# A sixteen-sequence linear-attention and local-attention kernel on one core: x in two buffers, the attention norm written over the turned rows, linear scores issued in fours, the layer input turned whole, set-up and main work in one block

## The chip, the cores and the metric

The kernel runs on one core of a Trainium2 chip. The metric is the device time of one execution in microseconds (us); smaller is better. The engines are named as the profile names them: PE (matrix products and the transposes done with them), PEld (its weight loads), DVE, ACT, POOL, and SP, which here only issues transfers.

## What is computed

The input x is 16 sequences of 512 rows and 128 columns. The reference, cut to what matters:

```python
# linear attention, 16 heads of 8
q, k, v = rope(x @ Wq.T), rope(x @ Wk.T), x @ Wv.T
q, k = elu(q) + 1, elu(k) + 1
y = causal_sum(q, k, v) / max(q . cumsum(k), 1e-6)
x = x + layernorm(y @ Wo.T)             # sandwich: x is normed ahead of it, too
# two layers, 8 heads of 64, windows of 64 looking one window back
for l in range(2):
    h = shift_token(x)                  # second half of the columns one row later
    q, k, v = split(h @ wqkv[l])
    q, k = rotary(l2norm(q) * qs, l2norm(k) * ks)
    x = x + softmax(mask(8 * q @ k.T)) @ v @ wo[l]
    h = layernorm(shift_token(x)) * g + b
    a, g = split(h @ w1[l] + b1)
    x = x + (a * gelu(g)) @ w2[l] + b2
```

The output is the residual after attention plus the norm of the layers' result.

## The kernel before, in words

Each sequence is four tiles (j = 0 to 3) of 128 rows. Its work is cut into steps, such as `yt` (four transposes of the normed x, L640), `aqkv` (L647), `as` (linear attention's scores, L679), `awo` (its output product, L705), `h` (the shifted layer input turned, L716 to L721), `qkv` (nine f16 products of 512 columns, L732), `qkt` (q and k turned, L744), `s` (window scores, L753 and L759), `pt` (probabilities turned, L771), `o` (L787), `wo` (L798), `w1` (L827) and `w2` (L838). A step has its part on other engines: copies out of the banks on ACT, rope, masks and norms on DVE, additions and normalising on POOL.

Nothing is scheduled while the kernel runs. A table `TIMES` gives every step of a sequence a number on each engine, `STARTS` gives each of the 16 sequences an offset, some 14,133 apart, and `order_of` sorts the sums: that is the order in which an engine issues. So four or five sequences are in flight, at different stages. Each engine takes its steps strictly in this order and waits on semaphores for what they need. The eight banks of 512 columns go to PE's steps by the table `HOLD` (`banks_of`), and `take` makes PE wait until the bank's last user has released it.

Set-up is a block of its own (L481 to L563): 38 loads on SP behind one semaphore, memsets on POOL, then, when all has landed, weights split into two f16 halves (ACT L533, DVE L545), the rope tables scaled (DVE L557), masks cast, and linear attention's weights turned (PE L525). Only when every engine has ended that block does the second block begin, with the first load of x (L588).

Around the change:

- `load` (L584) writes the one buffer `x_in`, so it waits until the sequence before has been kept (`x_kept`) and normed (`act_ln["mid"]`). Then come `ln_in` on DVE (L1047), `rstd` on POOL, `norm_in` on ACT (L867) into `y_rows`, and `yt` on PE.
- `norm_attn` (L1055) writes attention's normed output into `y_rows` too, and `add_mid` (L1253) adds it to x. So `norm_in` of a sequence waits for `add_mid` of the one before.
- `scores_linear` (L672) takes a bank and issues a product, four times.
- `h` (L709) makes the row shift on PE: one product that zeroes a column (L716), four that shift the upper half of the columns (L719), four transposes of the lower half (L721). One copy on ACT (L908) and one subtraction on DVE (L1131) then write the two f16 halves of `h_cols`.
- `expand` (L1271) writes one of two buffers `la_qexp`.

Of the kernel before, what the change touches and what calls it, by code (L numbers as in the profile page):

```python
# [91 lines left out]
class Step:  # L92
# [8 lines left out]
    def name(self):  # L101
# [3 lines left out]
STARTS = [8839, 22968, 37104, 51237, 65372, 79508, 93645, 107777, 121914, 136050, 150187, 164318, 178448, 192583, 206718, 220840]  # L105
TIMES = {
    "tensor": {
        "yt": [[4430]],
        "aqkv": [[5379, 5741, 5887, 6259]],
        "at": [[6260, 7486, 7515, 12974]],  # L110
        "aq": [[6500, 7904, 12992, 14314]],
        "as": [[9594, 9957, 14446, 14942]],
        "ao": [[10473, 10563, 14977, 15227]],
        "awo": [[15262]],
        "h": [[17736], [35934]],
        "qkv": [[17805, 20226, 20589, 21185], [38794, 39614, 41261, 43323]],
        "qkt": [[20484, 21053, 21367, 23845], [42226, 42333, 43672, 44789]],
# [8 lines left out]
    },  # L126
    "vector": {
        "ln_in": [[3336]],
        "arope": [[4897, 5228, 5494, 7780]],
        "phi": [[5339, 7394, 8144, 12251]],  # L130
        "den": [[6519, 8903, 12441, 14291]],
        "mask": [[10206, 11028, 15093, 15325]],
        "ln_attn": [[15539]],
        "norm_attn": [[16843]],
        "ln_mid": [[17151]],
        "h": [[18039], [38031]],
        "ss": [[18745, 20244, 21725, 23553], [40963, 41947, 43215, 43739]],
        "rope": [[19117, 21242, 22076, 22957], [41018, 42210, 43239, 44970]],
        "max": [[21946, 22977, 23802, 25207], [43513, 45053, 45539, 46335]],
# [43 lines left out]
        "r_ffn": [[29895], [51024]],  # L183
        "b2": [[29689], [53617]],
        "r_out": [[60936]],
        "add_out": [[67247]],
    },
    "sync": {
        "load": [[3648]],
# [1173 lines left out]
```

## Time and profile before

| | |
|---|---|
| median of 3 runs | 1835.49 us (1835.01 to 1836.9) |
| profiled execution, its own time | 1839.22 us |
| its span, first to last instruction | 1836.7 us, granted PE clock 0.971 |
| PE busy | 1641.0 us, 89% of the span |
| ACT, DVE, POOL busy | 1367.3, 1329.3, 1285.8 us |
| chain that ended last, by engine | PE 70%, ACT 12%, POOL 7%, issue 6%, DVE 3% |

The profiled execution is 3.7 us above the median of the runs, and 2.5 us of its time lie outside its span. Busy time says how much of the span an engine worked; a matrix product's end is modelled, so neighbouring products overlap in the rows, and what a step costs PE is best read from its start to the start of the next step.

### The profile page before, as it was taken

The numbers are of one execution on the slowest core, as the hardware profiler recorded it, in microseconds if no ns is written. First come the engines' busy times: TensorE is split into PE (matmuls) and PEld (weight loads), VectorE is DVE, ScalarE is ACT, GpSimd is POOL, SyncE is SP. The second block draws the span as 40 slices with busy tenths as digits, with TensorE's granted clock in tenths as the row PEclk, the third lists the DMA queues.
The fourth block names the chain that finished last, engine by engine and source line by source line (L and its number), as shares of the span: only waits on it lengthen the run. The fifth ranks groups of instructions, "written<-read, shape, count | busy, mean of one in ns | idle before, by whom it ended". The sixth has DMA issues, their size and how long they took to land.

```text
span 1836.7 us, 51372 instructions
## 1 busy us (share of the span) xinstructions
PE 1641.0 (89%) x18212; PEld 1149.2 (63%) x18340; DVE 1329.3 (72%) x3471; ACT 1367.3 (74%) x4277; POOL 1285.8 (70%) x1715
## 2 busy tenths in 40 slices
PE   0677989999999999999999999999999999998875
PEld 0344666666667666666666666666667666666653
DVE  2465777877777787877778787777777787776552
ACT  1264768787887878798887878787787878788663
POOL 1263777777777887777777787777777887777562
PEclk9888999999999999999999999999999999999986
DMA  3000001011111011111111011111101011111001
GB/s 117 12 16 19 22 23 25 18 36 30 36 28 28 19 34 27 31 36 30 36 28 28 19 31 30 31 36 28 39 22 31 22 25 36 30 31 30 19 21 29
DMA packets 58135, 54.52 MB, mean 30 GB/s; under 512 B 7538, under 2 KB 42780, under 8 KB 57756
## 3 DMA queue, kind: packets, MB, share of 16 engines
q1 hardware_dynamic: 57884, 51.25, 11.0%
q8 instruction: 149, 2.44, 0.5%
q14 instruction: 102, 0.84, 0.2%
HBM read 13.48 MB, written 8.39 MB: 12 GB/s over the span
## 4 chain that ended last, share of the span: by engine, by line
PE 70%; ACT 12%; POOL 7%; issue 6%; DVE 3%; DMA 0%; POOLq 0%; ACTq 0%; DVEq 0%; SPq 0%
PE bank L732 10%; PE bank L787 7%; PE bank L759 7%; PE bank L798 5%; PE bank L744 5%; PE bank L771 5%; PE bank L838 4%; PE bank L827 4%; PE bank L679 4%; PE bank L695 3%; PE bank L753 2%; PE bank L719 2%; ACT probs L959 2%; ACT probs_t L853 2%; POOL qk_rows L1308 2%
## 5 line engine op out<-in xcount | busy, mean ns | idle before, releaser
L959 ACT ACTIVATE probs<-bank,s_low 128x128 f32<-128x128 f32 x1024 | 360.1, 384 | 60.7 <-DVE s_low L1171 60.6
L1308 POOL TENSOR_TENSOR qk_rows<-qk_rows,qk_tmp 128x512 f32<-128x512 f32 x256 | 328.2, 1282 | 16.6 <-DVE qk_tmp L1159 15.8
L1321 POOL TENSOR_TENSOR probs<-probs,s_rden 128x512 f32<-128x512 f32 x256 | 263.5, 1050 | 68.1 <-DVE s_rden L1180 68.1
L732 PE MATMUL bank<-wqkv_sb,h_cols 128*128 128x512 f16 x1152 | 281.2, 388 | 7.9 <-ACT probs_t L853 2.6
L1311 POOL TENSOR_TENSOR qk_rows<-qk_rows,qk_rnorm 128x512 f32<-128x512 f32 x256 | 268.7, 1050 | 20.1
L959 ACT ACTIVATION_READ_ACCUMULATOR probs<-bank,s_low 128x1 f32 x1024 | 229.0, 224 | 0.0
L1156 DVE TENSOR_TENSOR qk_rows<-bank,rope 128x512 f32<-128x512 f32 x256 | 174.4, 681 | 39.2 <-POOL qk_rows L1311 35.4
L1126 DVE TENSOR_TENSOR room<-bank,const 128x512 f32<-128x512 f32 x256 | 158.7, 683 | 57.8 <-PE bank L679 56.2
L732 PEld LDWEIGHTS bank<-wqkv_sb,h_cols 128*128 128x128 f16 x1152 | 108.2, 99 | 142.7 <-issue 22.7
L853 ACT ACTIVATE probs_t<-bank 128x512 f32<-128x512 f32 x256 | 140.9, 598 | 67.9 <-PE bank L771 65.2
L1142 DVE TENSOR_REDUCE qk_sum<-qk_sq 128x16 f32<-128x1024 f32 x128 | 155.1, 1212 | 46.2 <-ACT qk_sq L918 44.2
L1171 DVE TENSOR_REDUCE s_low<-bank 128x4 f32<-128x512 f32 x256 | 164.3, 684 | 30.6 <-PE bank L759 30.6
L1159 DVE TENSOR_TENSOR qk_tmp<-bank,rope 128x512 f32<-128x512 f32 x256 | 174.3, 681 | 0.0
L918 ACT ACTIVATE qk_sq<-bank 128x512 f32<-128x512 f32 x256 | 144.4, 618 | 22.9 <-PE bank L732 22.2
L798 PE MATMUL bank<-wo_sb,o_cols 128*128 128x128 f32 x1024 | 141.0, 281 | 19.4 <-DVE room L1126 12.5
L744 PE MATMUL bank<-const,qk_rows 128*128 128x128 f32 x1024 | 140.8, 281 | 15.4 <-POOL qk_rows L1311 12.6
L798 PEld LDWEIGHTS bank<-wo_sb,o_cols 128*128 128x128 f32 x1024 | 129.5, 195 | 38.1 <-DVE room L1126 24.9
L771 PE MATMUL bank<-const,probs 128*128 128x128 f32 x1024 | 142.5, 280 | 8.8 <-POOL probs L1321 6.8
L787 PE MATMUL bank<-probs_t,v_even 128*64 128x64 f32 x2048 | 133.2, 228 | 17.6 <-ACT probs_t L853 10.1
L759 PEld LDWEIGHTS bank<-k_cols,q_cols 64*64 64x64 f32 x4096 | 112.3, 134 | 55.5 <-issue 55.5
L759 PE MATMUL bank<-k_cols,q_cols 64*64 64x128 f32 x4096 | 143.4, 278 | 0.0
L827 PE MATMUL bank<-h_cols,w_sb 128*128 128x512 f16 (+1 forms) x576 | 139.6, 386 | 2.1 <-ACT h_cols L990 0.9
(154 smaller groups left out, 3650.6 us busy)
## 6 DMA issues: line engine op xcount, KB each, us to landing
v_even<-v_rows SPq DMA_DIRECT2D x224, 128.0 KB, 2.3
x_in<-in_L_attn_x SPq DMA_DIRECT2D x16, 256.0 KB, 3.2
kept_rows<-x_in SPq DMA_DIRECT2D x16, 256.0 KB, 2.3
x_back<-kept_rows SPq DMA_DIRECT2D x16, 256.0 KB, 3.0
out<-x_back SPq DMA_DIRECT2D x16, 256.0 KB, 2.4
room<-in_constants SPq DMA_DIRECT2D x1, 1024.0 KB
hidden<-in_L_ffn_wqkv SPq DMA_DIRECT2D x1, 768.0 KB
qk_rows<-in_L_ffn_wqkv SPq DMA_DIRECT2D x1, 768.0 KB
```

The costliest lines, as they stand in the source:

```text
L732: mm = pe.matmul(to[:, :], h_cols[st.l][:, x_half, st.j * P:(st.j + 1) * P], wqkv_sb[:, st.l, w_half, w * INNER:(w + 1) * INNER], start=(n ...
L744: mm = pe.transpose(to[:, c * P:(c + 1) * P], qk_rows[st.l][:, a, w, c * P:(c + 1) * P], ident)
L759: mm = pe.matmul(to[half][w * WIN:(w + 1) * WIN, c * P:(c + 1) * P], q_cols[st.l][rows, a, c, w * WIN:(w + 1) * WIN], k_cols[st.l][rows, c ...
L771: mm = pe.transpose(to[:, c * P:(c + 1) * P], probs[st.l][:, half * PAIRS + c, :], ident)
L787: mm = pe.matmul(to[half * DH:(half + 1) * DH, c * P + w * WIN:c * P + (w + 1) * WIN], values[l][:, a, head * DH:(head + 1) * DH], probs_t ...
L798: mm = pe.matmul(to[:, 0:D], o_cols[st.l][:, c * P:(c + 1) * P], wo_sb[:, st.l, c, :], start=(c == 0), stop=(c == PAIRS - 1))
L827: mm = pe.matmul(to[0:n, :], w1_sb[:, st.l, w_half, half * HID + at_:half * HID + at_ + n], h2_cols[:, x_half, :], start=(p == 0), stop=(p ...
L853: return act.activation(to, of, ACT.Copy)
L959: act.activation(probs[st.l][:, n, :], bank[b[half]][:, c * P:(c + 1) * P], ACT.Exp, bias=s_low[st.l][:, a, n:n + 1], accum_out=s_sum[st.l ...
L1308: pool.tensor_tensor(rows(w), rows(w), qk_tmp[l][:, w, :], ALU.add).then_inc(pool_qk.of(st), 1)
L1311: pool.tensor_tensor(heads64(rows(w)), heads64(rows(w)), qk_rnorm[l][:, a, w * HEADS:(w + 1) * HEADS].unsqueeze(2).to_broadcast([P, HEADS, ...
L1321: pool.tensor_tensor(probs[l][:, mine, :], probs[l][:, mine, :], s_rden[l][:, a, mine].unsqueeze(2).to_broadcast([P, PAIRS, P]), ALU.mult) ...
```

## The change

What it does:

- `x_in` becomes two buffers, by the sequence's parity; `load` waits for the sequence two back.
- `norm_attn` writes into `y_cols` (seen by rows, `att_rows`), which `awo` has just read; `norm_in` then waits only for the last `yt`, and the copy that fills `y_cols` (`yt` on ACT) waits for the `add_mid` before.
- `scores_linear` takes its four banks first and then issues the four products; a step never gets one bank twice. `la_qexp` becomes one buffer, and `expand` waits for the tile before.
- `h` is four transposes of the whole 128 columns. The row shift is made where the bank is read: two copies on ACT and two subtractions on DVE, each of 64 partitions, the upper ones one column further. Column 0 is zeroed once.
- There is one block. x is loaded first, then what linear attention needs (5 loads, semaphore `first_loaded`), then layer by layer (`loaded[l]`). Splitting weights and scaling tables are called from within the engines' orders, in the first sequence. PE waits for `ready[l]` ahead of each layer's first `qkv`. Each engine sets the starting values of its own semaphores. The memsets write only what needs a zero.
- `STARTS`, `TIMES` and `HOLD` have new numbers throughout.

```diff
-STARTS = [8839, 22968, 37104, 51237, 65372, 79508, 93645, 107777, 121914, 136050, 150187, 164318, 178448, 192583, 206718, 220840]
+STARTS = [-1084, 13059, 27198, 41340, 55477, 69615, 83756, 97894, 112036, 126177, 140319, 154457, 168599, 182734, 196875, 211009]
...
-            b = min(range(BANKS), key=lambda b: (free[b], b))
+            b = min(set(range(BANKS)) - set(banks[step.name()]), key=lambda b: (free[b], b))
...
-        x_in = sb("x_in", [P, NT, D])
+        x_in = sb("x_in", [P, 2, NT, D])
...
+        att_rows = y_cols[:, :].rearrange("p (j d) -> p j d", j=NT)
...
-        la_qexp = room[:, 0:1024].rearrange("p (a s q) -> p a s q", a=2, s=SLOTS)
+        la_qexp = room[:, 0:512].rearrange("p (s q) -> p s q", s=SLOTS)
...
+        def start_signals(engine, mine):
+            for sig in every:
+                if sig.name.split("_")[0] in mine:
                     for sem in sig.sems:
-                        sp.sem_inc(sem, sig.start())
+                        engine.sem_inc(sem, sig.start())
...
-                    sp.wait_ge(*x_kept.at(st, back=1))
-                    sp.wait_ge(*act_ln["mid"].at(st, back=1))
-                    sp.dma_start(x_in[:, :, :], rows_of(x, st)).then_inc(x_loaded.of(st), 16)
+                    sp.wait_ge(*x_kept.at(st, back=2))
+                    sp.wait_ge(*act_ln["mid"].at(st, back=2))
+                    sp.dma_start(x_in[:, st.n % 2, :, :], rows_of(x, st)).then_inc(x_loaded.of(st), 16)
...
+                start_signals(sp, ("x", "out", "v", "sh"))
+                for at, (_, st) in enumerate(order["sync"]):
+                    if at > 0:
+                        run(st)
+                        continue
+                    sp.dma_start(x_in[:, 0, :, :], rows_of(x, st)).then_inc(x_loaded.of(st), 16)
+                    load_first()
+                    for l in range(DEPTH):
+                        load_layer(l)
+                    sp.wait_ge(zeroed, ZEROED)
...
                     pe.wait_ge(*pool_qexp.at(st))
+                    to = [take(banks, g) for g in range(GROUPS)]
                     for g in range(GROUPS):
-                        to = take(banks, g)
...
-                    pe.matmul(to[DH:P, 0:1], ident[:, DH:P], cst("causal")[:, 0:1], start=True, stop=True)
                     for j in range(NT):
-                        n = min(P, T - 1 - j * P)
-                        pe.matmul(to[DH:P, j * P + 1:j * P + 1 + n], x_res[st.l][0:n, j, DH:D], ident[0:n, 0:n],
-                                  start=True, stop=True)
-                        mm = pe.transpose(to[0:DH, j * P:(j + 1) * P], x_res[st.l][:, j, 0:DH], ident)
+                        mm = pe.transpose(to[:, j * P:(j + 1) * P], x_res[st.l][:, j, :], ident)
...
+                start_signals(pe, ("pe",))
+                pe.wait_ge(first_loaded, 16 * FIRST_LOADS)
+                for n in range(4):
+                    mm = pe.transpose(bank[0][:, n * D:(n + 1) * D], la_rows[:, n * D:(n + 1) * D], ident)
+                mm.then_inc(turned, 1)
+                pe.wait_ge(la_ready, 2)
                 for _, st in order["tensor"]:
+                    if st.kind == "qkv" and st.n == 0 and st.j == 0:
+                        pe.wait_ge(ready[st.l], READY[st.l])
...
                 def yt(st, b):
                     act.wait_ge(*pe_yt.at(st))
+                    act.wait_ge(*pool_xmid.at(st, back=1))
...
                 def norm_in(st, b):
-                    act.wait_ge(*pool_xmid.at(st, back=1))
+                    act.wait_ge(*pe_yt.at(st, back=1))
...
-                    copy(h_cols[st.l][:, 0, :], bank[b[0]][:, :]).then_inc(act_h.of(st), 1)
+                    copy(to[0:DH, 0, :], bank[b[0]][0:DH, :]).then_inc(act_h.of(st), 1)
+                    copy(to[DH:P, 0, 1:T], bank[b[0]][DH:P, 0:T - 1]).then_inc(act_h.of(st), 1)
...
-                    normed(st, "attn", lambda j: bank[b[0]][:, j * D:(j + 1) * D], lambda j: y_rows[:, j, :])
+                    normed(st, "attn", lambda j: bank[b[0]][:, j * D:(j + 1) * D], lambda j: att_rows[:, j, :])
...
-                    dve.tensor_tensor(h_cols[st.l][:, 1, :], bank[b[0]][:, :], h_cols[st.l][:, 0, :],
+                    dve.tensor_tensor(to[0:DH, 1, :], bank[b[0]][0:DH, :], to[0:DH, 0, :],
+                                      ALU.subtract).then_inc(dve_h.of(st), 1)
+                    dve.tensor_tensor(to[DH:P, 1, 1:T], bank[b[0]][DH:P, 0:T - 1], to[DH:P, 0, 1:T],
                                       ALU.subtract).then_inc(dve_h.of(st), 1)
...
+                    if st.name() == ("den", 0, 1, 0):
+                        lower_weights(0)
+                    if st.name() == ("mask", 0, 0, 0):
+                        turn_tables(0)
+                        turn_masks()
+                    if st.name() == ("mask", 0, 3, 0):
+                        lower_weights(1)
+                    if st.name() == ("ln_mid", 0, 0, 0):
+                        turn_tables(1)
...
-                    pool.wait_ge(*pe_as.at(st, back=2))
-                    pool.tensor_tensor(la_qexp[:, a, :, :],
+                    pool.wait_ge(*pe_as.at(st, back=1))
+                    pool.tensor_tensor(la_qexp[:, :, :],
```

`lower_weights`, `turn_tables` and `turn_masks` on DVE and `halve` on ACT hold the operations of the old set-up block unchanged, with semaphores. ACT calls `halve(0)` after `av` of the first sequence's last tile and `halve(1)` after its first `ao`.

On SP, the end of set-up and the first steps, before:

```order
L502 DMA room<-in_L_ffn_k_scale 128x64
L481 UNCONDITIONAL_BRANCH
L579 UNCONDITIONAL_BRANCH
L588 DMA x_in<-in_L_attn_x 128x4x128
L592 DMA kept_rows<-x_in 128x4x128
L588 DMA x_in<-in_L_attn_x 128x4x128
```

and now the start of the program on SP (its line numbers are the changed kernel's):

```order
L581 DMA x_in<-in_L_attn_x 128x4x128
L554 DMA o_cols<-in_L_attn_Wq 128x128
L554 DMA o_cols<-in_L_attn_Wk 128x128
L554 DMA o_cols<-in_L_attn_Wv 128x128
L554 DMA o_cols<-in_L_attn_Wo 128x128
L555 DMA const<-in_constants 128x708
L559 DMA hidden<-in_L_ffn_wqkv 128x1536
```

The first x went out last, behind the block's end; now it goes first, and five loads later PE may begin.

On PE, the layer input's `h` in the middle of the program, before (scores of a window ahead of it; the pair L719, L721 stands four times):

```order
L753 MATMUL bank<-mask_h,ident_h 128x512 x2
L759 MATMUL bank<-k_cols,q_cols 64x128 x16
L716 MATMUL bank<-const 64x1
L719 MATMUL bank<-const,x_res 64x128
L721 MATMUL bank<-const,x_res 64x128
```

and now (L711 and L717 are the window's scores, L609 `aqkv`, L729 `pt`, L679 `h`, L756 `wo`):

```order
L711 MATMUL bank<-mask_h,ident_h 128x512 x2
L717 MATMUL bank<-k_cols,q_cols 64x128 x16
L609 MATMUL bank<-w_la,y_cols 128x384
L729 MATMUL bank<-const,probs 128x128 x8
L679 MATMUL bank<-const,x_res 128x128 x4
L756 MATMUL bank<-wo_sb,o_cols 128x128 x4
```

Nine instructions became four, and `aqkv` of the next sequence (L609), which stood behind `h`, now stands ahead of it.

On PE, behind the first `qkv` of layer 0, before (L640 is `yt` and L647 `aqkv` of the next sequence, L771 `pt`):

```order
L732 MATMUL bank<-wqkv_sb,h_cols 128x512 x9
L640 MATMUL bank<-const,y_rows 128x128 x4
L771 MATMUL bank<-const,probs 128x128 x8
L647 MATMUL bank<-w_la,y_cols 128x384 x2
L787 MATMUL bank<-probs_t,v_even 64x64 x2
```

and now (L690 is `qkv` of tiles 0 and 1, L785 `w1`, L616 and L626 `at`, L756 `wo`, L729 `pt`, L609 the last `aqkv`; one `o` and then `qkt` of tile 0 follow):

```order
L690 MATMUL bank<-wqkv_sb,h_cols 128x512 x18
L785 MATMUL bank<-h_cols,w_sb 128x512 x6
L616 MATMUL bank<-la_phi,const 128x128
L626 MATMUL bank<-const,la_phi 128x128
L785 MATMUL bank<-h_cols,w_sb 128x512 x6
L756 MATMUL bank<-wo_sb,o_cols 128x128 x4
L729 MATMUL bank<-const,probs 128x128 x8
L785 MATMUL bank<-h_cols,w_sb 85x512 x6
L609 MATMUL bank<-w_la,y_cols 128x384
```

Between `qkv` and `qkt` of tile 0, `yt`, one `pt` and three `aqkv` have gone; all else that stood there still does.

## Rows read from the trace of the kernel before

**Rows 1.** Windows: stretch, length, busy us per engine, granted clock, DMA share, GB/s.

```profile
303.00:407.10 104.10, 99.71 (x1141) 70.64 (x1148) 80.36 (x211) 84.70 (x268) 78.74 (x106) 1.00 0.11 27
...
1447.60:1552.50 104.90, 99.82 (x1141) 70.64 (x1148) 82.00 (x215) 85.02 (x268) 80.03 (x108) 1.00 0.12 29
```

**Rows 2.** Waits of PE from 511 to 927 us: total, times, longest.

```profile
PE bank L640 <- ACT y_rows L864: 4.1, 4, 1.0
PE bank L798 <- DVE room L1126: 3.3, 4, 0.8
```

**Rows 3.** Timeline of PE, 600 to 720 us: start, length, instruction; both `h`.

```profile
627.01 0.28 PE L716 MATMUL bank<-const 128*64 128x1 f32 x2
...
629.50 0.34 PE L787 MATMUL bank<-probs_t,v_even 128*64 128x64 f32 x4
...
639.59 0.60 PE L815 MATMUL bank<-const,h_rows 128*128 128x128 f32 x4
640.12 1.14 PE L679 MATMUL bank<-room,la_qk_cols 32*128 32x512 f32 x8
...
691.97 0.28 PE L716 MATMUL bank<-const 128*64 128x1 f32 x2
...
694.36 1.06 PE L798 MATMUL bank<-wo_sb,o_cols 128*128 128x128 f32 x8
```

**Rows 4.** Groups by form, ACT and DVE, 511 to 927 us: busy, mean ns, idle.

```profile
L853 ACT ACTIVATE h_cols<-bank 128x512 f16<-128x512 f32 x8 | 4.8, 597 | 10.1 <-PE bank L721 10.1
L1134 DVE TENSOR_TENSOR h_cols<-bank,h_cols 128x512 f16<-128x512 f32 x8 | 5.5, 688 | 1.0 <-ACT h_cols L853 1.0
L1000 ACT ACTIVATE hidden<-bank,b_cols 128x512 f32<-128x512 f32 x16 | 10.1, 684 | 0.1
L1000 ACT ACTIVATE hidden<-bank,b_cols 85x512 f32<-85x512 f32 x8 | 5.5, 684 | 0.5
```

**Rows 5.** The start: one window, and two rows of the timeline.

```profile
0.00:10.00 10.00, 0.00 (x0) 0.00 (x0) 0.00 (x0) 1.28 (x1) 7.21 (x19) 1.00 0.84 291
...
35.68 0.38 SPq L588 DMA_DIRECT2D x_in<-in_L_attn_x  x1
...
43.24 1.11 PE L640 MATMUL bank<-const,y_rows 128*128 128x128 f32 x4 [19.20 <-ACT y_rows L864]
```

**Rows 6.** Timeline of set-up on DVE.

```profile
24.42 1.76 DVE L545 SCALAR_TENSOR_TENSOR wqkv_sb<-hidden,wqkv_sb 128x1536 f16<-128x1536 f32 x1 [1.25 <-ACT wqkv_sb L533]
...
26.09 0.86 DVE L545 SCALAR_TENSOR_TENSOR w_sb<-room,w_sb 128x682 f16<-128x682 f32 x1
...
30.31 4.39 DVE L557 SCALAR_TENSOR_TENSOR rope<-room 128x64 f32<-128x64 f32 x32
```

**Rows 7.** Timeline of DVE in the first sequence's linear attention.

```profile
57.74 4.88 DVE L1126 TENSOR_TENSOR room<-bank,const 128x512 f32<-128x512 f32 x8 [2.12 <-PE bank L679]
...
77.38 0.89 DVE L1027 BATCH_NORM_STATS2 ln_stats_attn<-bank 128x6 f32<-128x128 f32 x4 [3.11 <-PE bank L705]
```

**Rows 8.** Timeline of DVE, the norm of a later sequence's x.

```profile
693.11 0.87 DVE L1027 BATCH_NORM_STATS2 ln_stats_in<-x_in 128x6 f32<-128x128 f32 x4 [2.21 <-DMA x_in<-in_L_attn_x]
```

**Rows 9.** Timeline of PE and POOL behind the first `qkv` of layer 0.

```profile
699.11 1.04 PE L771 MATMUL bank<-const,probs 128*128 128x128 f32 x8
700.11 1.53 PE L647 MATMUL bank<-w_la,y_cols 128*128 128x384 f32 x4
...
702.65 0.91 PE L647 MATMUL bank<-w_la,y_cols 128*128 128x384 f32 x2
...
707.66 1.04 POOL L1311 TENSOR_TENSOR qk_rows<-qk_rows,qk_rnorm 128x512 f32<-128x512 f32 x1
...
711.96 1.04 PE L744 MATMUL bank<-const,qk_rows 128*128 128x128 f32 x8
```

**Rows 10.** One line of DVE: ns min/median/max over the run.

```profile
L1098 DVE SCALAR_TENSOR_TENSOR la_phi<-la_tb,la_phi x64: 361/519/1099, 50.4 to 1582.9; 128x256 f32<-128x256 f32 x64
```

**Rows 11.** Timeline of PE, a linear score step with a wait inside.

```profile
664.73 1.66 PE L679 MATMUL bank<-room,la_qk_cols 32*128 32x512 f32 x8
```

More of the change, by code:

```diff
@@ L102, in name @@
         return self.kind, self.l, self.j, self.n
-STARTS = [8839, 22968, 37104, 51237, 65372, 79508, 93645, 107777, 121914, 136050, 150187, 164318, 178448, 192583, 206718, 220840]
+STARTS = [-1084, 13059, 27198, 41340, 55477, 69615, 83756, 97894, 112036, 126177, 140319, 154457, 168599, 182734, 196875, 211009]
 TIMES = {
     "tensor": {
[L108 to L117, printed above, removed]
[8 rows of a table removed]
+        "yt": [[1158]],
+        "aqkv": [[2489, 2532, 2791, 6884]],
+        "at": [[4747, 8646, 9544, 9563]],
+        "aq": [[7014, 9242, 9578, 10422]],
+        "as": [[9363, 9420, 11127, 12264]],
+        "ao": [[9396, 9564, 14266, 14691]],
+        "awo": [[14736]],
+        "h": [[17531], [37133]],
+        "qkv": [[18557, 18868, 21223, 21826], [37717, 37818, 38228, 40867]],
+        "qkt": [[21050, 22007, 22211, 23528], [38284, 40531, 40869, 43385]],
[8 rows of a table added]
@@ new lines @@
+        "arope": [[4092, 4623, 5005, 7413]],
+        "phi": [[4675, 7364, 11296, 11633]],
+        "den": [[6477, 10514, 12784, 13983]],
+        "mask": [[10890, 11635, 15176, 15779]],
+        "ln_attn": [[17077]],
+        "norm_attn": [[17729]],
+        "ln_mid": [[17773]],
+        "h": [[18820], [39085]],
+        "ss": [[19735, 21000, 22082, 23183], [40148, 41353, 42710, 44412]],
+        "rope": [[20422, 21284, 22434, 24117], [40364, 41804, 43140, 44685]],
+        "max": [[22303, 24407, 25017, 26815], [43977, 44803, 46012, 46919]],
@@ L184 @@
-        "b2": [[29689], [53617]],
-        "r_out": [[60936]],
-        "add_out": [[67247]],
+        "r_in": [[937]],
+        "ar": [[2562, 2652, 2782, 6648]],
+        "aden": [[4262, 7986, 10959, 11311]],
+        "expand": [[7221, 9672, 11320, 11580]],
+        "r_attn": [[15507]],
+        "add_mid": [[16105]],
+        "r_mid": [[16458]],
+        "norms": [[18318, 19562, 20652, 21694], [38807, 39374, 40127, 43031]],
+        "normalize": [[18387, 20433, 20720, 23582], [39045, 39580, 42128, 43176]],
@@ L1010, in _, with halve @@
                 on_gelu = True
+                def halve(l):
+                    act.wait_ge(loaded[l], 16 * LOADS[l])
+                    for whole, halves in ((whole_wqkv[l], wqkv_sb[:, l, :, :]), (whole_w1[l], w1_sb[:, l, :, :])):
+                        act.activation(halves[:, 0, :], whole, ACT.Copy, scale=W_SCALE).then_inc(halved, 1)
+                start_signals(act, ("act",))
+                act.wait_ge(zeroed, ZEROED)
                 for _, st in order["scalar"]:
@@ new lines, in turn_tables @@
+                def turn_tables(l):
+                    for w, (names, by) in enumerate(((("q_cos", "q_sin"), QK_SCALE), (("k_cos", "k_sin"), 1.0))):
+                        sc = qk_scale[:, l, w, :].rearrange("p (a b) -> p a b", a=2)
+                        for c, name in enumerate(names):
+                            scales = sc[:, ::-1, :] if c else sc
+                            for j in range(NT):
+                                dve.scalar_tensor_tensor(
+                                    out=rope[:, l, 2 * w + c, j * DH:(j + 1) * DH].rearrange("p (a b) -> p a b", a=2),
+                                    in0=cst(name)[:, j * DH:(j + 1) * DH].rearrange("p (a b) -> p a b", a=2),
+                                    scalar=by, in1=scales, op0=ALU.mult, op1=ALU.mult).then_inc(ready[l], 1)
```

310 lines of the change are left out of this document (146 added, 164 removed), and 32 rows, old and new, of tables (HOLD, TIMES).

## The prediction

> **What bounds the kernel now.** I read the windows first, then PE's waits, then the timeline at the places that the change touches. In the windows, twelve sequences in a row, from 303 to 1552 us, take 104.0 to 104.9 us each, and PE is busy 99.7 to 99.8 us of that at a granted clock of 1.00, which is the upper of its two levels, 2.4 GHz [rows 1]. ACT works some 85 us of the same stretch, DVE 80 to 82, POOL 79 to 80 [rows 1]. So in the steady part PE's own work sets the pace. The 4.3 us in which it idles consist of small waits, and two of them have names: 1.0 us per sequence until the normed x of the next sequence is there, 0.8 us until DVE has masked linear scores ([rows 2], where each stands for four sequences). A microsecond taken from PE here is a microsecond per sequence, until another wait takes its place. The two ends of the run are another matter. PE turns the first x at 43.24 us [rows 5], after a set-up block and one load; there, chains of latency decide.
>
> **The change part by part.**
>
> *Start.* Now x is issued at 35.68 us and turned 7.56 us later [rows 5]. In the changed order x is SP's first transfer, and five loads follow it. Together they are 0.87 MB (256 KB of x, four weights of 64 KB, 128 rows of 708 constants), or 3.0 us at the 291 GB/s of the first ten microseconds [rows 5]. To the 7.56 us I add these 3.0, then 1.1 for turning linear attention's weights (the same four transposes took 1.11 cold [rows 5]) and 0.8 for two copies of them by DVE, an estimate from an ACT copy of as many columns [rows 4]. If x is issued at about 1.5 us, the first turn comes at 14: a lead of 29 us. I hold 26 to 31 possible, since what the engines spend on setting their semaphores has no row.
>
> *Set-up work within the first sequence.* It is no longer ahead of everything, but DVE still has to do it. Ahead of the first `h` stand both splits, 2 x (1.76 + 0.86), and half of the tables, 2.2 [rows 6], with some 1.5 us of small casts: 8.9 us. DVE waits in that stretch anyway, 2.1 us for the first scores and 3.1 us for `awo` [rows 7]. If the work fills these two holes, 3.7 us remain on the path; at best nothing does, at worst all 8.9. The second half of the tables comes after `ln_mid`, beside POOL's and ACT's share of that norm, and I cost it at nothing; without that cover it would be 2.2 us, once. I take 4, so the lead at the first `h` is **25 us** (17 to 31).
>
> One row bears on how long this work takes beside POOL: an operation of DVE with two inputs from SBUF takes 0.36 us at least, 0.52 in the middle and 1.10 at most over the run [rows 10]. The Trainium skill (SBUF — State Buffer, "Who interferes with whom") says that such an instruction contends with a POOL instruction that reads SBUF, the later one being blocked; the spread agrees. By that rule the moved operations, which had POOL idle beside them, would take longer now, by the middle of the row 0.16 us for each of about 20: 3 us more, inside the bounds above.
>
> *The layer input.* Nine PE instructions took 2.49 and 2.39 us from their first to the next step's first; four whole transposes of the same kind take 0.53 [rows 3]. That is 1.96 + 1.86 = 3.8 us of PE time less per sequence. In the twelve full periods all of it counts: 46 us. The other four sequences' eight steps fall where PE has gaps. There the path also gets what the split adds: a second copy on ACT, 0.60, and a second subtraction on DVE, 0.69 [rows 4]. Half the partitions do not halve these: ACT took 684 ns on 128 and on 85 of them [rows 4]. So each of the eight saves between 0.6 and 1.9 us; I take 1.2, together 10. Sum **56 us** (51 to 61). In the steady part the extra 1.2 us of ACT and 1.4 of DVE per sequence lie inside their 19 and 22 us of slack [rows 1]; what is queued behind them is in the next but one item.
>
> *Two buffers for x.* The wait of 1.0 us per sequence on PE [rows 2] ends a chain: DVE waited 2.2 us for x itself [rows 8], then come the norm on POOL and ACT. With a second buffer the load may go out one sequence earlier, and `norm_in` no longer waits for `add_mid`. In the new order `ln_in` also stands ahead of `ln_attn` of the sequence before. I expect this wait to go: 12 x 1.0 = **12 us** (0 to 12). The copy into `y_cols` now waits for `add_mid` instead, and holds `aqkv`; on PE, about ten steps stand between `awo` and that.
>
> *Handing over to `qkt`.* The order was laid out anew, and one place got tighter. Behind the first `qkv` of layer 0, POOL ended its normalising at 707.66 + 1.04 = 708.70, and PE came to `qkt` at 711.96 [rows 9]: 3.3 us to spare. From between them `yt`, one `pt` and three `aqkv` have been taken. These are 0.5 us (four transposes, as above), 1.0 (699.11 to 700.11) and 2.3 (two in 1.53, one in 0.91, overlaps taken off) [rows 9]: 3.8 us. What was 3.3 early is now 0.5 late, and ACT's second copy, which stands ahead of the squares, adds 0.6. I charge 1.2 us per sequence, 12 x 1.2 = **14 us**. Nothing at all is the lower bound, since POOL and ACT were reordered too; 3.8 + 0.6 = 4.4 us, 53 in all, is the upper one, if today's spare time is gone for another reason.
>
> *Linear scores.* Four products cost 1.14 us [rows 3]; a step that had to wait inside took 1.66 [rows 11]. Taking the banks first moves such a wait ahead of the products and changes nothing in the sum. The single `la_qexp` lets POOL's next expansion start only after the products; on PE, two other steps and an `ao` stand between two such steps, so I cost it at nothing. Without that cover it would be one addition-sized POOL operation, about a microsecond.
>
> **Sum.** -25 - 56 - 12 + 14 = -79 us against the profiled execution's 1839.2, so 1760. The median of the runs lies 3.7 us below that execution; I forecast **1756 us**, with 1738 to 1775 as this case's own range.
>
> **The rivals.**
>
> *The new handovers bind.* If `qkt` comes late by the full 4.4 us in every period, 3.2 us more than charged, the time is 1756 + 12 x 3.2 = 1794. For it speaks that ACT and POOL are 82% and 77% busy, so a chain through both seldom has its shortest length. Against it speaks that today's spare time is measured, 3.3 us [rows 9], and would have to be lost to other causes.
>
> *PE's other waits shrink as well.* Of 4.3 us of idle time per sequence 3.3 remain without the x wait. If half of that goes and the 1.2 us do not come, the time is 1756 - 12 x 2.8 = 1722. For it: PE's named waits now are all for masks, copies and norms that a new order can place earlier. Against it: the second copy and subtraction, and fewer PE steps to hide behind.
>
> *Four banks at once are not to be had: slower than before.* PE stands still until the fourth bank is free, with everything queued behind it. There are 64 such steps, 4 per sequence. It decides from a mean wait of 79 / 64 = 1.2 us. Its price at worst is a whole set of masks, 4.88 / 2 = 2.4 us [rows 7]: 64 x 2.4 = 156, so 1912. For it: the 0.5 us inside one step [rows 11] and the 0.8 us behind masks [rows 2] are waits of this kind. Against it: they are 1.3 us per sequence today, not 5.
>
> *The start gains nothing.* If the five first loads land only with all the rest, which is issued behind them on the same queue, PE begins no earlier in effect, and the 25 us are lost: 1781.
>
> **How the numbers follow.** Forecast 0.63, handovers 0.15, shrinking waits 0.13, banks 0.04, start 0.05. The range takes in the first two rivals' times and the start's, with a few microseconds beyond each: 1718 to 1800. A measurement of this kernel can tell about 0.2%, 3.7 us, from no change. Only the banks' case lies above that; the handovers would have to cost 6.4 us more per period than I charged to come near it. So 0.95 for faster, 0.01 for the same, 0.04 for slower.
>
> **What would show it.** Right: a first turn of x at 12 to 17 us; a period of 99 to 102 us with PE busy about 96; `h` at about 0.5 us on PE; no wait for the normed x; a new wait of a microsecond at the first `qkt`. Wrong: a period still near 104 with PE busy 96 (the work went, the time did not); PE waiting ahead of linear scores; a first turn after 20 us.

## The result and the profile after

The changed kernel takes **1748.56 us** (median of 4 runs, 1748.41 to 1750.26) against 1835.66 before (4 runs): a ratio of 0.9527, 95% interval 0.951 to 0.9543, 87.1 us less. The forecast was 1756, the range 1718 to 1800. The profiled execution took 1748.4, of which its span is 1746.6.

The page of the kernel after, its first and its fourth part (busy time of each engine; the chain that ended last, by engine):

```profile
PE 1575.0 (90%) x17892; PEld 1110.9 (64%) x18020; DVE 1375.7 (79%) x3503; ACT 1383.1 (79%) x4309; POOL 1292.7 (74%) x1717
...
PE 38%; ACT 27%; POOL 14%; issue 10%; DVE 10%; DMA 0%; POOLq 0%; SPq 0%; ACTq 0%; DVEq 0%
```

PE had 70% of that chain before; now ACT, POOL and DVE hold half of it. Windows of the kernel after, two of eleven equal ones in a row (columns as in [rows 1]):

```profile
337.37:438.22 100.85, 96.33 (x1121) 68.52 (x1128) 84.80 (x217) 85.88 (x270) 80.56 (x108) 1.00 0.12 31
...
1345.87:1446.72 100.85, 95.98 (x1120) 68.38 (x1127) 85.35 (x218) 85.46 (x271) 80.27 (x107) 1.00 0.12 31
```

Against [rows 1]: the period went from 104.1 to 100.85, PE's busy time from 99.7 to 96.0, its idle time from 4.4 to 4.8 (both traces lack the same few of PE's records; the last section has what that does to these two). PE's timeline after, both `h` (compare [rows 3]):

```profile
447.35 0.63 PE L679 MATMUL bank<-const,x_res 128*128 128x128 f32 x4 [0.52 <-ACT x_res L831]
447.92 1.16 PE L756 MATMUL bank<-wo_sb,o_cols 128*128 128x128 f32 x8
...
481.56 0.66 PE L679 MATMUL bank<-const,x_res 128*128 128x128 f32 x4
482.26 0.38 PE L711 MATMUL bank<-mask_h,ident_h 128*128 128x512 bf16 x1
```

From `h` to the next step it is 0.57 and 0.70 us, where it was 2.49 and 2.39. PE's waits from 438.1 to 943.4, five periods (compare [rows 2], which are four):

```profile
PE bank L690 <- DVE h_cols L1117: 4.4, 5, 1.1
PE bank L745 <- DVE room L1106: 4.0, 5, 0.8
PE bank L711 <- DVE room L1106: 2.8, 4, 0.8
PE bank L702 <- POOL qk_rows L1341: 2.5, 5, 0.5
PE bank L679 <- ACT x_res L831: 2.1, 4, 0.5
...
PE bank L641 <- DVE x_att L1168: 1.9, 5, 0.4
PE bank L641 <- ACT k_cols L819: 1.7, 5, 0.3
```

The wait for the normed x is gone. New are 0.9 us per sequence for the lower half of `h_cols` (`qkv`, L690), 0.5 for the normalised q and k (`qkt`, L702), and 0.7 for banks ahead of linear scores (`as`, L641). The masks (`room`) now hold up two steps, L745 and L711.

The start, from the timeline of several engines (compare [rows 5]):

```profile
1.79 0.44 SPq L581 DMA_DIRECT2D x_in<-in_L_attn_x  x1
...
12.88 1.28 ACT L831 ACT_TABLE_LOAD   x1 [12.88 <-POOL ln_nmr_in L1280]
14.18 1.65 ACT L831 ACTIVATE y_rows<-x_in,ln_nmr_in,ln_rstd_in 128x128 f32<-128x128 f32 x4
...
15.97 1.09 PE L602 MATMUL bank<-const,y_rows 128*128 128x128 f32 x4 [7.03 <-ACT y_rows L831]
...
69.93 0.63 PE L679 MATMUL bank<-const,x_res 128*128 128x128 f32 x4 [0.70 <-ACT x_res L831]
```

The first x is turned at 15.97 instead of 43.24.

Read so far, the two traces seem to bear the forecast out step by step: 3.7 us less on PE at `h`, 3.7 less busy time, a period 3.25 shorter. The experiments show that this reading is wrong in its main step.

For them one yardstick serves: when PE turns the x of a sequence (`yt`, from PE's timeline; the period is the time from the 5th turn to the 16th by 11).

| kernel | time, us | 1st turn | 2nd | 5th | 16th | period |
|---|---|---|---|---|---|---|
| before | 1835.7 | 43.2 | 97.3 | 386.7 | 1532.0 | 104.12 |
| after | 1748.6 | 16.0 | 62.4 | 337.4 | 1446.5 | 100.83 |
| 1. before + new `h` | 1817.5 | 42.8 | 95.4 | 379.9 | 1511.1 | 102.84 |
| 2. after + old `h` | 1769.3 | 16.1 | 62.5 | 340.9 | 1464.1 | 102.11 |
| 3. after, old numbers | 1810.7 | 16.0 | 76.3 | 362.0 | 1506.1 | 104.00 |
| 4. before + two x, one expansion buffer | 1854.1 | 42.4 | 96.7 | 385.3 | 1544.0 | 105.34 |
| 5. before + one expansion buffer | 1851.9 | 42.7 | 97.7 | 386.7 | 1545.2 | 105.32 |
| 6. after, set-up first | 1770.2 | 40.7 | 82.5 | 360.3 | 1469.8 | 100.86 |
| 7. after + more PE work | 1774.7 | 16.2 | 64.7 | 341.7 | 1467.5 | 102.35 |
| 8. after, one bank at a time | 1742.7 | 16.5 | 64.5 | 336.8 | 1442.0 | 100.47 |
| 9. after, earlier subtraction | 1743.6 | 16.3 | 64.3 | 334.9 | 1443.3 | 100.76 |
| 10. as 9, `qkv` regrouped, table first | 1748.6 | 14.9 | 61.3 | 333.0 | 1444.5 | 101.05 |
| 11. 8 and 9, table first | 1740.9 | 15.0 | 61.5 | 332.7 | 1438.5 | 100.52 |
| 12. as 11, one step moved | 1744.6 | 15.0 | 61.5 | 333.5 | 1442.6 | 100.83 |

### The profile page after: what moved, and what is told of

The parts are those of the page before. It is cut to its first block, busy times and chain, and to the rows that moved or that the text cites. A ratio compares the mean times of both kernels' runs of the same rounds, so it can differ in the third digit from the quotient of the medians.

```text
span 1746.6 us, 50872 instructions
## 1 busy us (share of the span) xinstructions
PE 1575.0 (90%) x17892; PEld 1110.9 (64%) x18020; DVE 1375.7 (79%) x3503; ACT 1383.1 (79%) x4309; POOL 1292.7 (74%) x1717
## 4 chain that ended last, share of the span: by engine, by line
PE 38%; ACT 27%; POOL 14%; issue 10%; DVE 10%; DMA 0%; POOLq 0%; SPq 0%; ACTq 0%; DVEq 0%
ACT probs L928 8%; PE bank L690 5%; POOL qk_rows L1341 5%; POOL qk_rows L1338 5%; PE bank L717 4%; PE bank L641 4%; DVE room L1106 3%; PE bank L785 3%; PE bank L745 3%; PE bank L702 3%; PE bank L657 3%; PE bank L756 3%; PE bank L729 3%; ACT probs_t L819 3%; ACT h_cols L819 2%
## 5 line engine op out<-in xcount | busy, mean ns | idle before, releaser
L1338 POOL TENSOR_TENSOR qk_rows<-qk_rows,qk_tmp 128x512 f32<-128x512 f32 x256 | 332.8, 1300 | 8.6 <-DVE qk_tmp L1142 8.5
L690 PE MATMUL bank<-wqkv_sb,h_cols 128*128 128x512 f16 x1152 | 277.6, 386 | 20.7 <-DVE h_cols L1117 14.9
L928 ACT ACTIVATION_READ_ACCUMULATOR probs<-bank,s_low 128x1 f32 x1024 | 240.8, 235 | 0.0
L690 PEld LDWEIGHTS bank<-wqkv_sb,h_cols 128*128 128x128 f16 x1152 | 105.7, 99 | 167.6 <-issue 38.3
L702 PE MATMUL bank<-const,qk_rows 128*128 128x128 f32 x1024 | 141.9, 278 | 23.6 <-POOL qk_rows L1341 22.0
L729 PE MATMUL bank<-const,probs 128*128 128x128 f32 x1024 | 142.2, 277 | 8.9 <-POOL probs L1351 8.3
L717 PEld LDWEIGHTS bank<-k_cols,q_cols 64*64 64x64 f32 x4096 | 112.5, 135 | 55.5 <-issue 55.5
L745 PE MATMUL bank<-probs_t,v_even 128*64 128x64 f32 x2048 | 132.5, 228 | 16.9 <-DVE room L1106 12.1
L756 PE MATMUL bank<-wo_sb,o_cols 128*128 128x128 f32 x1024 | 143.9, 284 | 2.9 <-ACT o_cols L819 2.9
L702 PEld LDWEIGHTS bank<-const,qk_rows 128*128 128x128 f32 x1024 | 114.4, 142 | 47.7 <-issue 34.3
L717 PE MATMUL bank<-k_cols,q_cols 64*64 64x128 f32 x4096 | 143.8, 279 | 0.0
L745 PEld LDWEIGHTS bank<-probs_t,v_even 128*64 128x64 f32 x2048 | 105.9, 137 | 55.4 <-DVE room L1106 24.5
```

What stands on the lines that cost most here:

```text
L690: mm = pe.matmul(to[:, :], h_cols[st.l][:, x_half, st.j * P:(st.j + 1) * P], wqkv_sb[:, st.l, w_half, w * INNER:(w + 1) * INNER], start=(n ...
L702: mm = pe.transpose(to[:, c * P:(c + 1) * P], qk_rows[st.l][:, a, w, c * P:(c + 1) * P], ident)
L717: mm = pe.matmul(to[half][w * WIN:(w + 1) * WIN, c * P:(c + 1) * P], q_cols[st.l][rows, a, c, w * WIN:(w + 1) * WIN], k_cols[st.l][rows, c ...
L729: mm = pe.transpose(to[:, c * P:(c + 1) * P], probs[st.l][:, half * PAIRS + c, :], ident)
L745: mm = pe.matmul(to[half * DH:(half + 1) * DH, c * P + w * WIN:c * P + (w + 1) * WIN], values[l][:, a, head * DH:(head + 1) * DH], probs_t ...
L756: mm = pe.matmul(to[:, 0:D], o_cols[st.l][:, c * P:(c + 1) * P], wo_sb[:, st.l, c, :], start=(c == 0), stop=(c == PAIRS - 1))
```

## The experiments

**1 and 2. The layer input by itself, in either order.** Experiment 1 puts the diff of `h` (PE, ACT, DVE, its two signals, the zeroed column) into the kernel before; 2 takes it out of the kernel after:

```diff
 # 1; and the reverse in 2
-    pe.matmul(to[DH:P, 0:1], ident[:, DH:P], cst("causal")[:, 0:1], start=True, stop=True)
     for j in range(NT):
-        n = min(P, T - 1 - j * P)
-        pe.matmul(to[DH:P, j * P + 1:j * P + 1 + n], x_res[st.l][0:n, j, DH:D], ident[0:n, 0:n], ...)
-        mm = pe.transpose(to[0:DH, j * P:(j + 1) * P], x_res[st.l][:, j, 0:DH], ident)
+        mm = pe.transpose(to[:, j * P:(j + 1) * P], x_res[st.l][:, j, :], ident)
```

Expected of 1: 

> The kernel before, in its old order, with the whole-turned layer input alone. If PE's own work sets the period, 3.8 us per sequence go and little comes back as waits: a period of 100.3 to 101, a time of 1780 to 1795. If the new order is what carries the gain, the freed time turns into waits here: a period above 102.5 and a time above 1812.

Expected of 2: 

> The changed kernel, in its new order, with the old layer input (nine instructions on PE, one copy, one subtraction). If the layer input's PE time is worth what it takes in a period, the period is 104 to 104.9 and the time 1788 to 1806. If PE no longer sets the period and the chain through ACT and POOL does, under half comes back: below 1775.

Measured (in brackets, here and below, the ratio to the kernel before and its 95% interval): 1 takes 1817.5 (0.9904, 0.9885 to 0.9922), 18.1 us less; 2 takes 1769.3 (0.9641, 0.9624 to 0.9657), 20.8 more than the kernel after. The period moves by **1.28 us** in both orders, for 3.7 us of PE's instructions. In both the second theory's numbers hold. PE's waits in 1, over five periods (L729 is `qkv`, L768 `pt`, L795 `wo`, L641 `yt`):

```profile
PE bank L729 <- DVE h_cols L1136: 7.0, 5, 1.7
PE bank L795 <- DVE room L1125: 4.0, 5, 0.8
PE bank L768 <- ACT v_rows L937: 3.4, 5, 0.7
PE bank L795 <- ACT o_cols L850: 3.1, 5, 0.6
...
PE bank L641 <- ACT y_rows L861: 0.6, 3, 0.2
```

1.4 us per sequence come back at the product that needs the lower half, 1.3 more behind ACT's copies. The wait for the normed x, 1.0 per sequence before, has all but gone here, with one buffer for x as before; 4 and 5 come back to that. In the new order, the way from the norm to that product, in the kernel after:

```profile
445.43 1.78 ACT L831 ACTIVATE x_res<-x_in,ln_nmr_mid,ln_rstd_mid 128x128 f32<-128x128 f32 x4
...
448.70 1.28 ACT L819 ACTIVATE h_cols<-bank 64x512 f16<-64x512 f32 x2
...
450.72 0.69 DVE L1117 TENSOR_TENSOR h_cols<-bank,h_cols 64x511 f16<-64x511 f32 x1
...
451.47 0.82 PE L690 MATMUL bank<-wqkv_sb,h_cols 128*128 128x512 f16 x3 [0.77 <-DVE h_cols L1117]
```

and in experiment 2 (L678 is the first of the nine products):

```profile
450.55 1.78 ACT L835 ACTIVATE x_res<-x_in,ln_nmr_mid,ln_rstd_mid 128x128 f32<-128x128 f32 x4
452.47 0.25 PE L678 MATMUL bank<-const 128*64 128x1 f32 x2 [0.52 <-ACT x_res L835]
...
455.04 0.60 ACT L823 ACTIVATE h_cols<-bank 128x512 f16<-128x512 f32 x1 [0.96 <-PE bank L683]
456.47 0.68 DVE L1116 TENSOR_TENSOR h_cols<-bank,h_cols 128x512 f16<-128x512 f32 x1
```

From the norm's start to the last subtraction's end it is 5.98 us now and 6.60 with the old `h`. PE comes to its next step 1.8 earlier, but ACT comes to the copy only 0.7 after that, and its second copy and DVE's second subtraction add 0.68 and 0.69. (With the old `h`, DVE came 0.8 after the copy.) The chain gains 0.62 of PE's 1.8, and PE waits 0.77 at its end. That is layer 0; layer 1's step is some 1.9 shorter. How the period's 1.28 splits over the two is not settled: experiment 9 makes this chain 0.38 shorter (5.60) and the wait at its end 0.35, and its period moves by 0.07 only.

**3. All code, none of the new numbers.** The kernel after with `STARTS`, `TIMES` and `HOLD` of before.

> The changed kernel with the three tables (offsets, times, bank holds) of the kernel before: every code change, none of the new order. If the sum of the prediction is right (start 25, layer input 56, x 12, each by code), the time lies between 1742 and 1762. If the new order carries a part, above all in the fill, where the second sequence's first turn came 35 us early, it is 1770 or more.

Measured: 1810.7 (0.9866, 0.9849 to 0.9882): 24.9 below before, 62.1 above the kernel after, and with a period of 104.00 not one microsecond better than before in its steady part. The second theory holds, and by more than it said: the new order, charged with +14 in the forecast, carries 62 of the 87 us. Some 14 of them are there by the second sequence's turn (76.3 against 62.4), 3.2 come in each period. So in the old order the code's parts cancel in the period: -1.28 for `h` (1) and +1.2 for the expansion buffer (5), -0.12 measured for all together. PE's waits in 3, five periods (L729 is `pt`, L756 `wo`, L641 `as`, L602 `yt`):

```profile
PE bank L729 <- ACT v_rows L907: 3.4, 5, 0.7
PE bank L756 <- ACT o_cols L819: 3.1, 5, 0.6
PE bank L641 <- ACT la_qk_cols L819: 2.8, 5, 0.6
PE bank L641 <- DVE h_rows L1176: 2.7, 5, 0.7
PE bank L602 <- ACT y_rows L831: 2.3, 5, 0.5
```

None of these five, 2.9 us per sequence, stands in the list of the kernel after; new there are, above all, the masks ahead of L711, `qkt` and the banks ahead of `as`, some 1.8. In 3 PE is busy 97.2 us a period and idle 6.8; in experiment 6, which has the new order and no missing records, it is busy 96.8 and idle 4.1. So the order took out waits for the most part, and hardly any work. Which of the three tables brings this, and which steps in them, was not tried.

**4 and 5. What two x buffers and one expansion buffer cost in the old order.** Experiment 4 takes over both; 5 the second alone:

```diff
-        la_qexp = room[:, 0:1024].rearrange("p (a s q) -> p a s q", a=2, s=SLOTS)
+        la_qexp = room[:, 0:512].rearrange("p (s q) -> p s q", s=SLOTS)
...
-                    pool.wait_ge(*pe_as.at(st, back=2))
+                    pool.wait_ge(*pe_as.at(st, back=1))
```

Expected of 4: 

> The kernel before, in its old order, with two buffers for x, attention's norm in the turned rows' buffer and the single expansion buffer that makes room for them; the layer input as before. If the 1.0 us wait for the normed x is a loss of its own, it goes: 1820 to 1827. If PE's next wait takes its place, or the copy that now waits for the residual addition does, the time stays within 1832 to 1838.

Expected of 5: 

> The kernel before, in its old order, with the single expansion buffer alone (one x buffer, old layer input). The run with two buffers for x, which had the single expansion buffer too, took 1854. If POOL's wait there for the linear scores, 2.2 us per sequence, is what it lost, this takes as long: 1848 to 1857. If the loss came from the second x buffer and the copy that waits for the addition, this stays at 1833 to 1838.

Measured: 4 takes 1854.1 (1.0099, 1.0084 to 1.0114), 5 takes 1851.9 (1.0092, 1.0071 to 1.0113). 4 fell out of both its theories, since it was slower; 5 names the cause. Here is the wait that it brought to POOL, over five periods of 5, and the same wait in the kernel after:

```profile
POOL room L1276 <- PE bank L679: 10.8, 5, 2.2
```

```profile
POOL room L1306 <- PE bank L641: 10.3, 5, 2.2
```

The single expansion buffer, costed at nothing, makes POOL wait 2.2 us per sequence with everything behind it on its queue, and the period grows by 1.2: some 16 us. The second x buffer gains nothing in the old order: 4 and 5 have the same period, and PE waits 1.0 us for the normed x in both. DVE's wait for x, 11.8 us over five periods before, is off its list in 4, so it was not what PE waited for. The trace of the kernel before shows what was:

```profile
694.56 0.60 ACT L853 ACTIVATE h_cols<-bank 128x512 f16<-128x512 f32 x1 [1.45 <-PE bank L721]
...
695.82 0.20 POOL L1250 TENSOR_TENSOR ln_nmr_in<-ln_nmr_in,ln_rstd_in 128x4 f32<-128x4 f32 x1
...
696.86 1.65 ACT L864 ACTIVATE y_rows<-x_in,ln_nmr_in,ln_rstd_in 128x128 f32<-128x128 f32 x4
...
698.65 0.63 PE L640 MATMUL bank<-const,y_rows 128*128 128x128 f32 x4 [1.03 <-ACT y_rows L864]
```

POOL's share of the norm ends at 696.02, but ACT comes to `norm_in` only at 696.86, without a pause since its copy for `h`, for which it had waited 1.45 us until PE's nine products ended. With the new `h` in 1, the wait goes from 1.0 to 0.1.

In the new order the second x buffer can't be taken out by itself, since `ln_in` of the next sequence stands ahead of `ln_attn` there and would wait for itself; and the single expansion buffer is what makes room for it. Neither was tried, so what POOL's 2.1 us cost in the kernel after stays open.

**6. Set-up first.** x is loaded after all the rest of the set-up, which ACT and DVE do ahead of their orders:

```diff
-                    sp.dma_start(x_in[:, 0, :, :], rows_of(x, st)).then_inc(x_loaded.of(st), 16)
                     load_first()
                     for l in range(DEPTH):
                         load_layer(l)
                     sp.wait_ge(zeroed, ZEROED)
+                    for l in range(DEPTH):
+                        sp.wait_ge(ready[l], READY[l])
+                    sp.dma_start(x_in[:, 0, :, :], rows_of(x, st)).then_inc(x_loaded.of(st), 16)
+                    sp.wait_ge(*x_loaded.at(st))
```

> The changed kernel with all of the set-up ahead of the first load of x, as in the kernel before, but in one block. If the earlier start reaches the end of the run, this costs what the lead at the first layer input was, 17 to 28 us: 1766 to 1777. If the fill or later waits had taken the lead back anyway, it costs under 5 us: below 1754.

Measured: 1770.2 (0.9644, 0.963 to 0.9658), 21.7 us more than the kernel after: the first theory. Of the 24.8 at the first turn, 22.9 are left at the fifth, and the period is the same. The start is a gain of its own and keeps to the end.

**7. A price for PE's work.** The normed x is turned five times over, into the same bank:

```diff
-                    for j in range(NT):
-                        mm = pe.transpose(to[:, j * P:(j + 1) * P], y_rows[:, j, :], ident)
+                    for _ in range(5):
+                        for j in range(NT):
+                            mm = pe.transpose(to[:, j * P:(j + 1) * P], y_rows[:, j, :], ident)
```

> The changed kernel with the normed x turned five times over instead of once: 16 more transposes on PE per sequence, 2.1 us by the four in 0.53, away from every copy that PE waits for in the steady part. If a microsecond of PE's work is a microsecond of the period, the period grows by 2.1 and the time by 26 to 34, to 1775 to 1783. If PE's waits in other places shrink for it, as the two runs on the layer input suggest (1.28 of 3.7), the period grows by 0.7 to 1.0 and the time lies between 1757 and 1766.

Measured: 1774.7 (0.9661, 0.9645 to 0.9676), 26.1 more. The period grows by 1.51. But the added work is not the 2.1 us expected; here is `yt` and PE's next step in 7, then in the kernel after:

```profile
546.84 2.35 PE L603 MATMUL bank<-const,y_rows 128*128 128x128 f32 x20
549.02 1.04 PE L730 MATMUL bank<-const,probs 128*128 128x128 f32 x8
```

```profile
539.10 0.60 PE L602 MATMUL bank<-const,y_rows 128*128 128x128 f32 x4
539.54 1.08 PE L729 MATMUL bank<-const,probs 128*128 128x128 f32 x8
```

From start to start it is 2.18 against 0.44, so some 1.75 us more per sequence, and a microsecond of PE costs 0.87 here: nearly the first theory's rule, with less work than it reckoned. At `h` it brought 0.35 (1.28 of 3.7), and in 2, where the work is put back, it cost as little. So away from `h`, PE's work is still most of the bound, which the second theory of 2 denied. That `h` is apart because new copies and subtractions stand behind its saving fits the waits of 1 and 2, but no run has the one without the other.

**8. One bank at a time.**

```diff
-                    to = [take(banks, g) for g in range(GROUPS)]
                     for g in range(GROUPS):
+                        to = take(banks, g)
```

> The changed kernel with linear scores taking one bank at a time again. By the prediction this changes nothing: 1745 to 1752. If PE loses time by waiting for the fourth bank ahead of the first product, it is faster by up to 0.75 us per sequence, 12 us: 1737 to 1744. If the copies behind it gain from the products issued together, it is slower by over 4 us.

Measured: 1742.7 (0.9496, 0.9481 to 0.9511), 5.9 less than the kernel after, the period 0.36 shorter. PE's two waits ahead of `as` (L641) are gone from its list; `qkt` waits 0.8 us per sequence now instead of 0.5. Taking the four banks before the first product costs time here.

**9 to 12. Towards a faster kernel.** 9 lets DVE begin after ACT's first copy:

```diff
-                    dve.wait_ge(*act_h.at(st))
+                    dve.wait_ge(*act_h.at(st, 1))
                     dve.tensor_tensor(to[0:DH, 1, :], bank[b[0]][0:DH, :], to[0:DH, 0, :],
                                       ALU.subtract).then_inc(dve_h.of(st), 1)
+                    dve.wait_ge(*act_h.at(st))
```

> The changed kernel, in which DVE's first subtraction for the layer input waits for ACT's first copy alone and no longer for both. The wait of PE for the second subtraction is 0.9 us per sequence; the subtractions end 0.6 us earlier. If that wait is a loss of its own, 12 x 0.5 = 6 us go: 1740 to 1745. If another wait stands right behind it, nothing: 1747 to 1750.

10 adds to that, in the first tile's `qkv`, all six products with the upper half ahead of the three with the lower, and an early load of ACT's table:

> As the run before, and the first tile's qkv issues all six products with the upper half ahead of the three with the lower half (three banks taken at once), and ACT loads its first table ahead of its first wait. If PE's wait for the lower half is a loss of its own, all 0.9 us per sequence go, and 1.3 us at the start: 1735 to 1741. If the three banks are not free at once, or the squares of the first tile come late because of it, it is no better than the run before, or worse.

11 is 8 and 9 with the early table load:

```diff
+                act.preload_act_table_set("gelu_and_others")
                 start_signals(act, ("act",))
```

> The changed kernel with the two edits that were faster, one bank at a time and DVE's first subtraction after ACT's first copy, and ACT's first table loaded ahead of its first wait. If the gains add up: 5.9 + 5.0 + 1.4, so 1735 to 1739. If they are the same waits seen twice: 1740 to 1743.

12 changes one number more, to put `o` of tile 1, layer 0, ahead of the first `as` of the next sequence on PE: `"o"` 23523 becomes 23503. The gaps in `STARTS` are not equal (14,134 to 14,143), and sorted with them, `o` comes ahead in 8 of the 15 places and stays behind in 7.

> As the run before, and on PE the output product of tile 1 of layer 0 ahead of the first linear scores, behind which it waited 0.8 us per sequence for one of their banks. If that wait is a loss of its own: 7 to 9 us below the run before. If the scores, now a microsecond later, are waited for by DVE and then by PE, no gain, within 3 us of the run before, or slower.

Measured: 9 takes 1743.6 (0.9497, 0.948 to 0.9514). The time is what the first theory said, the place is not: the period is 0.07 shorter, and 2.5 us of the gain are there by the fifth turn. 10 takes 1748.6 (0.9524, 0.9505 to 0.9544), 5 more than 9 in the median (one of its four runs, at 1743.8, was as fast) although its first turn came 1.4 earlier: PE now waits 1.3 us per sequence for the lower half, against 0.7 in 9. 11 takes **1740.9** (0.9477, 0.9462 to 0.9492): better than both kernels, 7.7 us below the kernel after, but the three gains do not add up (5.9 + 5.0 + 1 would have been 1737), and against 8 alone the intervals overlap. 12 takes 1744.6 (0.9499, 0.9485 to 0.9513): of five periods, `qkt` waits for masks in three and `o` still does in two, and nothing was won. What it brings to move `o` in every sequence was not tried.

## Why the prediction was right in its sum and wrong in its terms

| term | forecast | measured | by |
|---|---|---|---|
| start | -25 | -21.7 | 6 |
| layer input | -56 | -18.1 and -20.8 | 1, 2 |
| two x buffers | -12 | none in the old order | 4 against 5 |
| single expansion buffer | 0 | some +16 in the old order | 5 |
| four banks first | 0 | +5.9 | 8 |
| new order (all three tables) | +14 | -62.1 | 3 |

- **The layer input** is the step that failed: "In the twelve full periods all of it counts: 46 us". It counted a third: PE's busy time fell by 3.6 us (101.1 in 5, 97.4 in 1), and 2.3 came back as idle time. The instructions shrank as forecast (0.57 and 0.70 us), and the added evictions took what they should: 643 and 592 ns on ACT, 681 and 693 on DVE. But that they "lie inside their 19 and 22 us of slack" was the wrong question: slack over a period says nothing of a queue of work that PE waits for at its end.
- **The order** was looked at in one place, for one loss. That loss came, smaller: `qkt` waits 0.5 us per sequence, not 1.2. What a new order can gain was a rival ("PE's other waits shrink", 1722), priced at 2.8 us a period against the forecast. The order brings 3.2, nearly all of the 3.3 by which the period fell.
- **Two x buffers**: the chain was read wrong. That DVE waited 2.2 us for x is so, but PE's wait ended with ACT, which came late to `norm_in` from the old `h` (4 and 5). So most of the 12 us was part of what `h` brings, and was counted a second time.
- **Why the sum held** was luck. The errors of +36 at the layer input, of +12, +16 and +6 at the buffers and banks, of +3 at the start and of -76 at the order cancel to a few microseconds (they were taken from different orders, so they need not add up exactly). A right total and a right period did not show a right working; taking single parts out did.
- **The start** was right at the first turn: forecast at 14, found at 15.97. Of the difference 1.28 us are a table load that ACT now does between the norm's last value and `norm_in`; before, it lay beside the set-up. The sum counted the lead at the first `h`, 25 (17 to 31). There it is 17.6, 69.93 against this row of the kernel before:

```profile
87.57 0.34 PE L716 MATMUL bank<-const 128*64 128x1 f32 x2 [10.23 <-ACT x_res L864]
```

  Of the lead of 24.8 against experiment 6 there are 21.1 left at the first `h` (91.02 there): the set-up work inside the first sequence cost 3.7, forecast at 4. The other 6 us by which the way from turn to `h` grew (44.3 before, 50.3 in experiment 6) come with the rest of the change; with which part of it is open. At the end of the run experiment 6 is 21.7 behind; it keeps the one block, and its first turn, at 40.75, is itself 2.5 ahead of before's.
- **The set-up's own operations** were expected to take longer beside POOL. Two of them and a POOL operation beside them, timelines of the kernel after:

```profile
29.23 1.74 DVE L1232 SCALAR_TENSOR_TENSOR wqkv_sb<-hidden,wqkv_sb 128x1536 f16<-128x1536 f32 x1
30.89 0.86 DVE L1232 SCALAR_TENSOR_TENSOR w_sb<-probs,w_sb 128x682 f16<-128x682 f32 x1
...
29.26 2.76 POOL L1315 TENSOR_TENSOR la_phi<-la_phi,la_rden 128x128 f32<-128x128 f32 x1 [0.74 <-DVE la_rden L1099]
```

  DVE's took 1.74 and 0.86, as in [rows 6]; POOL's took 2.76 instead of 0.41 (its median over the run), began 0.03 after DVE's and ended 0.27 after the second. It lies on the chain that ended last, so the price was paid, 2.35 us, by the other engine. In experiment 3 an operation of POOL had begun first:

```profile
28.41 0.72 POOL L1298 TENSOR_TENSOR la_ta<-la_ta,la_tb 128x256 f32<-128x256 f32 x1
...
28.67 2.08 DVE L1232 SCALAR_TENSOR_TENSOR wqkv_sb<-hidden,wqkv_sb 128x1536 f16<-128x1536 f32 x1
```

  There DVE's first took 2.08, 0.34 longer. The Trainium skill (SBUF — State Buffer, "Who interferes with whom") says that a DVE instruction with two SBUF inputs contends with a GpSimd (here POOL) instruction that reads SBUF, and that the order of issue decides which of the two blocks; both traces agree. In the kernel after, the prediction had the two engines the wrong way round.
- **The rival that would have made it slower** (four banks not to be had) was right in kind and far off in size: PE does wait ahead of `as`, 0.7 us per sequence where 5 would have been needed.

## What to carry to other kernels

Where engines run fixed orders, price a saved microsecond by the chain that it lies on: a microsecond of the same engine was worth 0.35 at a step with new copies behind it, and 0.87 at transposes away from them. Count a second buffer's loss (here the expansion's) by who stands behind the new wait on that queue, and never cost a new order by one place alone. When a change has several parts, take each out before believing a sum that fits.

## What the runs showed of the hardware beyond that

A trace can lack records of PE, and its busy time with them. Eleven periods each of before, of 5, of 1 and of 6:

```profile
386.66:1532.03 1145.37, 1097.28 (x12519) 777.26 (x12607) 906.28 (x2354) 933.17 (x2938) 879.74 (x1167) 1.00 0.12 30
```

```profile
386.69:1545.16 1158.47, 1111.57 (x12607) 777.32 (x12607) 905.14 (x2354) 934.77 (x2938) 880.74 (x1168) 1.00 0.12 29
```

```profile
379.91:1511.13 1131.22, 1071.86 (x12386) 758.66 (x12387) 920.52 (x2377) 946.50 (x2960) 881.08 (x1167) 1.00 0.12 30
```

```profile
360.31:1469.79 1109.48, 1064.61 (x12388) 753.15 (x12387) 934.77 (x2377) 943.92 (x2960) 885.26 (x1167) 1.00 0.12 31
```

In 5, 1 and 6 PE has as many records as PEld, to one or two. In before 88 are missing, eight per sequence, all of them of the masks' product (L753, 128 records in the whole trace where that of 5 has 256). The traces of the kernel after and of 2, 8, 9 and 10 lack the same. Where none is missing, PE's busy time goes with its instructions and hardly with the order: 101.1 us a period with the old `h` (4 and 5), 97.4 and 97.2 with the new one in the old order (1 and 3), 96.8 in the new order (6). The granted clock is 1.00 in all. So `h` took its time out of PE's busy time in full (3.6 us between 5 and 1, 3.7 by its steps), and what came back, and what the orders change, is idle time: 5.4 us a period in 1, 6.8 in 3, 4.1 in 6. For before it is 3.1, if its products take what they take in 5; the 4.4 of [rows 1] have the missing records in them.

PEld's busy time is 70.7 us a period in before and in 5 alike. The Trainium skill (Perfetto Trace Analysis, "Identifying the Most-Contended Engine") says that the busy share of matrix products is not a good measure, because pipelined instructions look smaller, and takes that of the weight loads instead, beside the arithmetic done. These rows agree that the weight loads are the steadier measure; that records are missing is another reason than the page's.

Half the partitions cost an eviction as much as all of them: ACT's copies of 64 took 643 and 592 ns, 597 on 128 [rows 4]. One load of ACT's tables took 1.28 us. In the three runs with the load ahead of the first wait (10 to 12) the first turn came at 14.9 to 15.0; in the six others that load x first it came at 16.0 to 16.5.
